# CoPE attention in a decoder layer: the selection in two row groups of 64 rows, its digits as bytes in buffers of their own

## The reference

```python
logits = einsum('bhqd,bhkd->bhqk', Q, K) / sqrt(32)
gates = sigmoid(logits)
pos = flip(cumsum(flip(gates, -1), -1), -1)        # how many gates lie at or behind key k
pos = minimum(pos, 63)
logits_int = einsum('bhqd,dn->bhqn', Q, pos_emb)   # 64 positions
cope = ceil/floor entries of logits_int at pos, interpolated by pos - floor(pos)
out = softmax(logits + cope) @ V
```

## Time and profile before

| | |
|---|---|
| time, median of 3 runs | 14364.57 us (14324.61 to 14424.61) |
| profiled execution | 14339.96 us |
| its span | 14338.3 us |
| mean granted TensorE clock | 0.859 |
| CoPE tiles | 512, from about 3704 to 13556 us of the span |

### The profile page before, as it was taken

How to read it: one execution, slowest core, us unless ns; L and a number is a source line. 1 busy time by engine, 2 the same in 40 slices (tenths; PEclk the granted TensorE clock), 3 DMA queues, 4 the chain that set the end, 5 groups by cost and what they waited for, 6 DMA issues and landing times. The chain is left out here.

```text
span 14338.3 us, 175721 instructions
## 1 busy us (share of the span) xinstructions
PE 11781.3 (82%) x56950; PEld 8123.5 (57%) x56950; DVE 7370.4 (51%) x13140; ACT 4442.6 (31%) x7890; POOL 6522.6 (45%) x5384
## 2 busy tenths in 40 slices
PE   8777999966688888888888888888888888888746
PEld 4554333344466666666666666666666666666522
DVE  0112444422466666666666666666656666665543
ACT  0111333311233333333333333333333333333210
POOL 0000000000466666666666666666666666666500
PEclk9888999977788888888888888888888888888766
DMA  3112222211333333333333333333333333333223
GB/s 75 52 44 55 75 76 75 75 59 65 71 77 85 77 79 84 78 81 83 80 80 84 79 80 85 79 80 83 78 83 80 78 85 79 78 86 78 65 71 102
DMA packets 1054792, 1096.90 MB, mean 77 GB/s; under 512 B 738818, under 2 KB 846082, under 8 KB 989202
## 3 DMA queue, kind: packets, MB, share of 16 engines
q1 hardware_dynamic: 981010, 1087.81, 31.1%
q10 hardware_dynamic: 73728, 8.42, 0.4%
HBM read 884.93 MB, written 210.76 MB: 76 GB/s over the span
## 5 line engine op out<-in xcount | busy, mean ns | idle before, releaser
L921 PE MATMUL c_pickps<-c_table,c_hot 128*128 128x112 f32 x16384 | 3467.2, 388 | 557.6 <-DVE c_over L1212 534.6
L921 PEld LDWEIGHTS c_pickps<-c_table,c_hot 128*128 128x128 f32 x16384 | 3297.9, 265 | 662.5 <-DVE c_over L1212 562.4
L1302 POOL TENSOR_TENSOR c_total<-c_total,c_over 128x384 f32<-128x384 f32 (+3 forms) x3584 | 3295.5, 919 | 467.2 <-DVE c_over L1212 187.4
L1189 DVE COPY_PREDICATED c_pickps<-c_upper,c_pickps 128x256 f32<-128x256 uint32 (+1 forms) x1024 | 798.9, 826 | 3349.8 <-PE c_pickps L921 3349.8
L1302 POOL TENSOR_TENSOR c_total<-c_total,c_middle 128x1024 f32<-128x1024 f32 x512 | 1210.6, 2364 | 2848.5 <-DVE c_middle L1203 2848.5
L1269 POOL IOTA c_digitrow<- 1x128 f32 x1 | 0.3, 256 | 3600.7 <-POOLq L65 3600.7
L1054 ACT ACTIVATE c_over<-c_place,c_thresholds 128x384 f32<-128x384 f32 (+3 forms) x3584 | 1589.2, 526 | 0.0
L1037 ACT ACTIVATE c_place<-c_gateps 128x512 f32<-128x512 f32 x1024 | 611.6, 597 | 2673.4 <-PE c_gateps L894 2673.3
L1212 DVE TENSOR_TENSOR c_over<-c_over,c_pickps 128x384 f32<-128x384 f32 (+3 forms) x3584 | 1407.1, 452 | 0.0
L894 PE MATMUL c_gateps<-c_qa,c_ka 128*128 128x512 f32 x2048 | 1105.2, 622 | 65.8 <-ACT c_place L1037 65.1
L960 PEld LDWEIGHTS c_softps<-c_v,c_probs 128*128 128x128 f32 x8192 | 1070.1, 209 | 138.7 <-issue 105.7
(11 more groups left out here) (213 smaller groups left out, 13625.0 us busy)
## 6 DMA issues: line engine op xcount, KB each, us to landing
c_hot<-t_digits SPq DMA_DIRECT2D x512, 1024.0 KB
t_tables<-c_tablesb SPq DMA_DIRECT2D x256, 256.0 KB, 5.8
c_table<-t_tables SPq DMA_DIRECT2D x1024, 56.0 KB, 2.3
a_q<-t_qa SPq DMA_DIRECT2D x64, 512.0 KB
a_k<-t_ka SPq DMA_DIRECT2D x64, 512.0 KB
c_kb<-t_kb SPq DMA_DIRECT2D x256, 128.0 KB, 6.9
t_digits<-c_anchorrows SPq DMA_DIRECT2D x128, 256.0 KB, 2.3
a_q<-t_qa SPq DMA_DIRECT2D x128, 128.0 KB, 2.4
```

What stands on the lines that cost most here:

```text
L921: mm = nc.tensor.matmul(pick_ps[:, h // 4, 0:WIDTH, r * 8:(r + 1) * 8], hot[t % 2][:, h, :], table[s][:, :, :, t * 16 + h].rearrange("p l ...
L1189: ins = nc.vector.copy_predicated(pick_ps[:, :, at:at + width, :], far.unsqueeze(2).to_broadcast([128, 4, width, 32]), pick_ps[:, :, at + ...
L1302: nc.gpsimd.tensor_tensor(a, a, b, ALU.add).then_inc(s_add, 1)
```

## The change

Four things, all in the CoPE stage:

1. **Selection in two row groups.** Each of the 16 products of a pick becomes two, on partitions 0 to 63 (lanes 0 to 3) and 64 to 127 (lanes 4 to 7). Each has 64 rows and 4 x 14 = 56 columns and writes banks of its own (0 and 1, or 2 and 3), the queries 8 apart.
2. **Digits as bytes, in buffers of their own.** `anchor_rows` and the DRAM scratch are bytes; `load_hot` writes the new byte buffer `digits`, and `compare` reads it and writes `hot`. load_hot therefore waits for the compare that read the buffer (`s_hot`), not for the pick.
3. **Layouts that follow.** `near` writes the anchor in two instructions in place of one, `keep_table` copies in four in place of one.
4. The order of scores and softmax is as before.

```diff
-        anchor_rows = sb("c_anchorrows", [128, QUAD])
+        anchor_rows = sb("c_anchorrows", [128, QUAD], U8)
+        digits = [sb(f"c_digits{x}", [128, 16, 128], U8) for x in range(2)]
...
             def load_hot(i, s, t):
                 x = t % 2
-                after(sp, s_pickps, 4 * i + t - 1)
+                after(sp, s_hot, 4 * i + t - 1)
...
-                sp.dma_start(hot[x][:, :, :], src).then_inc(s_hotload[x], 16)
+                sp.dma_start(digits[x][:, :, :], src).then_inc(s_hotload[x], 16)
...
                 for h in range(16):
                     if h == 8 and turn is not None:
                         turn_anchor(turn)
-                    r = h % 4
-                    mm = nc.tensor.matmul(pick_ps[:, h // 4, 0:WIDTH, r * 8:(r + 1) * 8], hot[t % 2][:, h, :],
-                                          table[s][:, :, :, t * 16 + h].rearrange("p l m -> p m l"), start=True, stop=True)
+                    for g in range(2):
+                        rows, lanes = slice(64 * g, 64 * g + 64), slice(4 * g, 4 * g + 4)
+                        mm = nc.tensor.matmul(pick_ps[:, 2 * g + h // 8, 0:WIDTH, h % 8:32:8], hot[t % 2][rows, h, :],
+                                              table[s][rows, lanes, :, t * 16 + h].rearrange("p l m -> p m l"),
+                                              start=True, stop=True)
                 mm.then_inc(s_pickps, 1)
...
-                nc.scalar.activation(table_sb[n][:, :].rearrange("p (l x) -> p l x", l=8), gate_ps[:, :].rearrange("p (x l) -> p l x", l=8),
-                                     ACT.Copy).then_inc(s_tablesb, 1)
+                kept = table_sb[n][:, :].rearrange("p (g l t e h) -> p g l t e h", g=2, l=4, t=4, e=2)
+                made = gate_ps[:, :].rearrange("p (t g e l h) -> p g l t e h", t=4, g=2, e=2, l=4)
+                for g in range(2):
+                    for e in range(2):
+                        ins = nc.scalar.activation(kept[:, g, :, :, e, :], made[:, g, :, :, e, :], ACT.Copy)
+                ins.then_inc(s_tablesb, 1)
...
-                nc.vector.tensor_scalar(anchor[:, :].rearrange("p (t l h) -> p t h l", t=4, l=8),
-                                        rounded[:, :].rearrange("p (t h l) -> p t h l", t=4, l=8), EIGHTS, None, ALU.subtract).then_inc(s_anchor, 1)
+                turned = anchor[:, :].rearrange("p (b l e h) -> p b l e h", l=4, e=2, h=8)
+                plain = rounded[:, :].rearrange("p (b e l h) -> p b l e h", l=4, e=2, h=8)
+                for e in range(2):
+                    ins = nc.vector.tensor_scalar(turned[:, :, :, e, :], plain[:, :, :, e, :], EIGHTS, None, ALU.subtract)
+                ins.then_inc(s_anchor, 1)
...
-                nc.vector.tensor_scalar(hot[x][:, :, :], hot[x][:, :, :], digit[:, :], None, ALU.is_equal).then_inc(s_hot, 1)
+                nc.vector.tensor_scalar(hot[x][:, :, :], digits[x][:, :, :], digit[:, :], None, ALU.is_equal).then_inc(s_hot, 1)
...
-    digit_rows, table_rows = scratch("t_digits", [2, 4, 128, 128]), scratch("t_tables", [2, 256, QUAD])
+    digit_rows, table_rows = scratch("t_digits", [2, 4, 128, 128], U8), scratch("t_tables", [2, 256, QUAD])
```

More of the change, by code:

```diff
@@ L7 @@
 U32 = mybir.dt.uint32
+U8 = mybir.dt.uint8
 ALU = mybir.AluOpType
@@ L1662, in build_decoder_layer, with scratch @@
 def build_decoder_layer(nc, a):
-    def scratch(name, shape):
-        return nc.dram_tensor(name, shape, F32).ap()
+    def scratch(name, shape, dt=F32):
+        return nc.dram_tensor(name, shape, dt).ap()
     xn_rows, ctx_rows, x1_rows, att_rows, x2_rows = (scratch(f"t_{n}", [ROWS, D]) for n in ("xn", "ctx", "x1", "att", "x2"))
```

## The result

| | before | after |
|---|---|---|
| median of 4 runs each | 14349.14 us (14324.61 to 14424.61) | 14774.15 us (14748.02 to 14844.67) |
| profiled span | 14338.3 us | 14774.6 us |
| mean granted clock | 0.859 | 0.764 |

The ratio is 1.0285, interval 1.0246 to 1.0323. The change makes the kernel 2.9% slower; forecast were 1.6% and 14,600 us in a range from 13,800 to 15,100. The sign, the range and the cause hold. The size is short by 174 us, and the sum came that near partly because terms missed on both sides.

The account below looks back on a forecast made before the run. Pick and DVE taking turns on the one-buffer pick_ps bound the kernel. Terms made a quad 78.9 us, 1.9 over 76.97; times 128, 245 us on 14340 gives 14585, with the median's offset about 14,600 us; range 13,800 to 15,100.

Parts of the forecast that it names:

- additions at the low clock, before `top`: PE's L939 passes at 1.2 GHz in each tile after a low pick: 1.3 us charged of 1.7 possible.
- compare: DVE's compare reading bytes, writing f32: taken at 1.28 us, no added cost; upper bound 1.03 us more a tile.
- pick of t=0, and its gate product at the low clock: Tile t=0: pick 2.2 us shorter, first gate product 0.9 us longer at the low clock.
- t=2: turned anchor, second half of the pick: Tile t=2: 0.7 us more for the turned anchor at low clock, 0.3 for the pick's wholly low second half.
- t=3: digits, keep_table, tables and values: Tile t=3: mean digit stall of 3.1 us gone, keep_table 0.5 more, tables and values at low clock 1.0 more.
- 4.1 us at the high clock: Pick of 64 passes in two row groups at 2.4 GHz: 64 x 0.058 + 0.37, against 6.33 before.
- Rival (d): Pick's row groups do not overlap, or scattered output slows passes: 0.11 us a pass, 15,600 us; chance 0.09.
- Rival (a): Clock holds through every pick: 66.0 us a quad, about 12,960 us; chance 0.10.
- the second loop: Loop over POOL beside the pick: gather_up, total added to scores, `top`; 15.74 us, next in line when the pick shrinks.
- a pick begun at 1.2 GHz lasts 7.0 us and has little reason to raise the clock: Low picks gain nothing, 7.0 us as before in the plain tile; clock returns only inside the L939 passes behind.
- Rival (c): DVE's compare runs one element at a time: 1.03 us more a tile, about 15,000 us; chance 0.12.
- POOL and DVE busy times as before: Sign of a right forecast in the profile after: both engines' busy times stay unchanged.

Follow-up runs that it names:

- filled_light: Changed kernel with logits on 128 rows, plus unread 216-column products ahead of values, four at t=2 and two at t=3: 13963.65 us, ratio 0.9736.
- experiments 3 to 6: Changed kernel with logits on 128 rows, 14495.72 us; with unread filler products added in three amounts, 14123.65, 13963.65 and 13908.51 us.
- whole_rows: Changed kernel with its 64 passes of 56 columns each reading all 128 rows, one after the other: 17249.85 us, ratio 1.2013.

## Why the prediction was right, and where its size was off

Per quad, forecast against the table above:

| step | forecast | measured |
|---|---|---|
| additions at the low clock, before `top` | 3 x 1.3 = +3.9 | 3 x 1.7 = +5.1 |
| stall of PE behind the pick | not seen | +0.8 |
| compare | 0 (bound 1.03 a tile) | +1.13 |
| pick of t=0, and its gate product at the low clock | -2.2 and +0.9 | -2.5 and -0.1 |
| t=2: turned anchor, second half of the pick | +1.0 | +0.5 in the pick, +0.55 ahead of it |
| t=3: digits, keep_table, tables and values | -3.1 + 0.5 + 1.0 = -1.6 | -2.3 from `top` on, without the compare |
| sum | +1.9 | +3.1 |

- **The pick.** "4.1 us at the high clock" is 3.81, and "7.0 us" at the low one is 7.08. Rival (d), groups that do not overlap or outputs that slow a pass, falls with 0.060 us a pass. Rival (a)'s bound for the second loop was too firm: I gave t=1 15.7 us by the POOL loop, and in filled_light, with a quick pick, it takes 14.70, behind a t=0 of 18.27 in which, as I read it, POOL can get ahead.
- **The clock.** The step that carried the sign held: "a pick begun at 1.2 GHz lasts 7.0 us and has little reason to raise the clock". All 329 slow picks end at 0.50, though 148 of them were begun at 2.4 GHz, which I had not foreseen, and rival (a)'s 12,960 us were never near, though experiments 3 to 6 took part of the way. The Trainium skill, "TensorE: Matmul & The Clock Gate", Part 1, would have had the clock up in picks without a gap; the trace does not agree, with 3.50 of 3.50 us busy at 0.50 here and 7.00 of 7.00 in whole_rows. The row that I read against it beforehand, 3.63 of 3.80 us busy, is weaker than I took it for: the clock falls at 8046.2, inside it, and in the stretch ahead of it, from 8041.00 to 8043.60, PE was busy for only 2.00 of 2.60 us. The rows of the slow picks do not have this weakness. My reason, that half as much goes through the array, is contradicted by no run and isolated by none; my experiment on the height alone missed that the columns were halved too.
- **The term that failed most** is "I charge 1.3 of the possible 1.7 us". The possible was the true one: the first two L943 passes do not bring the clock back, and all four run low. That is 1.2 us a quad, or 154 us, nearly the whole gap of 174.
- **The compare** had the right bound for the wrong reason. Rival (c) asked whether a byte source runs one element at a time. It does not (1.28 us in most tiles). The cost came from POOL, with +1.13 a quad, and, through the late `base`, from the clock. The forecast "POOL and DVE busy times as before" missed it too: DVE's rose by 195 us, of which 147 are compares ((1638 - 1350) ns x 512). In the earlier trace rows the 2310 ns were there to be asked about: I called them rare and did not look up what POOL did beside them.
- **The gate product of t=0.** Its 0.9 us were a step too many. The product stands beside DVE's wait for the additions, which I had charged already; from `top` on the tile gets shorter, not longer (-0.11 with both pieces).
- **t=3.** The stall of the digits went as said (8.7 us are left of 416 over the whole execution). keep_table costs 0.79 us for 0.60, 0.2 more where I took 0.5. The tables and values at the low clock are hidden for the most part behind DVE.
- **The stall of PE** stood nowhere in the sum. It is worth 0.8 us a quad, about 100 us, and the code of the picks doubling was in plain view in the diff.

Over and under then cancel: 3.1 us too little in the first three rows, 2.0 too much in the other three, 1.2 net with the rounding.

## What to carry to other kernels

Cutting a product into smaller ones that run side by side shortens it only where the clock stays high (6.33 to 3.81 us here, and 7.0 to 7.1 at 1.2 GHz); look at what fills the stretch ahead of it and whether its own passes will bring a low clock back, and if not, charge every pass behind it at 1.2 GHz in full. The gains of two edits that act on the same wait are not to be summed: here the bytes were worth 348 us alone and about nothing beside the row groups, so time each alone before they are joined. The parts to keep here are the bytes and the wider logits (13,854 us against 14,774 for the change as made).

## What the runs showed of the hardware that I had not expected

- Picks of 56-column passes at full height, begun at 0.50, stood there for 13.9 us of gapless work (0.217 us a pass; 0.114 at 2.4 GHz); the L921 passes of 112 columns brought the clock back.
- A compare of 2048 elements takes 1.28 or 2.1 to 2.4 us, by whether it or POOL's addition starts first, and POOL's addition of 512 elements 1.27 or 2.24; 0.3 us of wait in DVE's queue decides.
- Twice as many passes in a pick took the packets of instructions from 28 to 644, and with quick passes PE stood for 1.5 us once per loop body, at its first instruction, which waits for nothing that the profile shows.
- PSUM outputs 32 bytes apart cost no time that these rows show: 0.060 us a pass. What would hide under the weights' pace (0.114 us a pass in whole_rows, with the same outputs) is not shown.
